# Gated cross-attention block with a quantised FFN: seven instead of six of the eleven products of a pair on Pool

## The reference, cut to what matters

```python
# x: (8, 512, 256); ctx: (8, 512, 256)
x = x + tanh(g_xattn) * attention(layernorm(x), ctx)      # 16 heads of 16, RoPE
xq   = fake_quant(layernorm(x))                           # one scale for the whole tensor
gate = xq @ wq(w_gate).T                                  # (4096, 704)
up   = xq @ wq(w_up).T                                    # (4096, 704)
h    = fake_quant(silu(gate) * up)                        # one scale: max|h| over everything
x    = x + tanh(g_ffn) * (h @ wq(w_down).T)
```

## Time and profile before

| | us |
|---|---|
| median of 3 executions | 604.42 (602.25 to 606.8) |
| the profiled execution, its own time | 602.7 |
| its span, first to last instruction | 600.9 |
| stage 2 of the FFN in it, first silu (514.43) to the last maximum's start (566.93) | 52.5 |
| busy in the span: PE, DVE, ACT, POOL | 565.9, 533.6, 442.1, 253.7 |
| mean granted TensorE clock | 0.995 |

### The profile page before, as it was taken

One profiled execution on the slowest core, in us unless ns is written; L12 is line 12 of the kernel. 1 busy time (PEld: TensorE's weight loads), 2 busy tenths in 40 slices (PEclk: granted clock), 3 DMA queues, 4 the chain that ended last, 5 costly groups with the idle time before them and its releaser, 6 DMA issues. The chain is left out here.

```text
span 600.9 us, 18561 instructions
## 1 busy us (share of the span) xinstructions
PE 565.9 (94%) x6592; PEld 262.3 (44%) x6592; DVE 533.6 (89%) x693; ACT 442.1 (74%) x873; POOL 253.7 (42%) x371
## 2 busy tenths in 40 slices
PE   7999999998899989999999999999999989888985
PEld 3655655233344434444444444444444433333364
DVE  4799989999999979899899899899899775799888
ACT  2667667257777877797797797798798672788694
POOL 8599989701333434214214215215214311665400
PEclk8999999999999999999999999999999999999999
DMA  8759887542332334233333234235222000000035
GB/s 290 242 161 302 244 189 214 139 104 69 73 76 60 73 65 73 53 84 76 53 75 84 53 69 89 53 64 86 62 62 48 3 2 0 2 2 0 0 106 176
DMA packets 61255, 55.21 MB, mean 92 GB/s; under 512 B 11040, under 2 KB 58784, under 8 KB 61216
## 3 DMA queue, kind: packets, MB, share of 16 engines
q1 hardware_dynamic: 61216, 54.70, 36.2%
HBM read 37.62 MB, written 16.78 MB: 91 GB/s over the span
## 5 line engine op out<-in xcount | busy, mean ns | idle before, releaser
L908 ACT ACTIVATE prob<-st_ps 128x512 f32<-128x512 f32 x512 | 280.7, 597 | 71.3 <-PE st_ps L765 64.2
L765 PE MATMUL st_ps<-q,k 98*32 98x512 bf16 x2048 | 178.9, 380 | 6.1 <-ACT prob L908 4.9
L968 DVE TENSOR_REDUCE negm<-xT_ps 128x2 f32<-128x1024 f32 x128 | 154.6, 1207 | 8.4 <-PE xT_ps L338 7.8
L968 DVE TENSOR_REDUCE negm<-v_ps 128x2 f32<-128x1024 f32 x128 | 154.4, 1206 | 6.3 <-PE v_ps L338 6.3
L789 PE MATMUL pv_ps<-prob,v_u 128*32 128x512 f32 x1024 | 132.8, 592 | 0.7 <-ACT prob L908 0.7
L765 PEld LDWEIGHTS st_ps<-q,k 98*32 98x32 bf16 x2048 | 56.9, 95 | 96.3 <-ACT prob L908 41.1
L338 PE MATMUL xT_ps<-k,q 96*32 96x512 bf16 x1024 | 78.4, 379 | 1.4 <-DVE negm L968 1.3
L338 PE MATMUL v_ps<-k,q 96*32 96x512 bf16 x1024 | 78.4, 380 | 1.1 <-DVE negm L968 1.0
L1157 POOL TENSOR_TENSOR msplit<-negm,onesf 128x16 bf16<-128x16 f32 x32 | 7.1, 223 | 129.8 <-DVE negm L968 129.8
L1177 POOL TENSOR_TENSOR normal<-turned,recip 128x256 f32<-128x256 f32 x32 | 19.9, 622 | 78.7 <-DVE recip L982 78.7
L789 PEld LDWEIGHTS pv_ps<-prob,v_u 128*32 128x32 f32 x1024 | 31.8, 110 | 25.8 <-issue 2.0
(11 more groups left out here) (153 smaller groups left out, 807.6 us busy)
## 6 DMA issues: line engine op xcount, KB each, us to landing
qk_parts<-parts SPq DMA_DIRECT2D x96, 128.0 KB, 2.7
k<-qk_parts SPq DMA_DIRECT2D x192, 64.0 KB, 2.7
q<-qk_parts SPq DMA_DIRECT2D x192, 64.0 KB, 3.0
ctx<-in_ctxT SPq DMA_DIRECT2D x8, 512.0 KB, 4.7
X<-in_x SPq DMA_DIRECT2D x8, 512.0 KB, 8.5
out<-X SPq DMA_DIRECT2D x7, 512.0 KB, 2.9
q<-mrow SPq DMA_DIRECT2D x64, 4.0 KB, 2.6
wf<-in_w_down SPq DMA_DIRECT2D x1, 704.0 KB, 5.0
```

What stands on the lines that cost most here:

```text
L765: last = nc.tensor.matmul(score_bank(i)[lo:lo + COLS, :], k6[g][:, h, kt * P + lo:kt * P + lo + COLS], q6[g][:, h, :], start=True, stop=True)
L908: nc.scalar.activation(prob[kt % 2][:, h, :], score_bank(HPU * kt + h)[:], ACT.Exp, scale=SCALE).then_inc(exp_done, 1)
L968: nc.vector.tensor_reduce(negm[g % 2][:, lo:lo + 2], pair[:], op=ALU.max, axis=AX.X, negate=True).then_inc(mx_read, 1)
```

## The change

Slot 4 moves from Pool to DVE, slots 3 and 5 move from DVE to Pool. Pool slots before: 0 2 4 6 8 9; now: 0 2 3 5 6 8 9. DVE slots before: 1 3 5 7 10; now: 1 4 7 10. Over the four pairs that is 24 to 28 copies on ACT, 24 to 28 products on Pool, and 20 to 16 products on DVE.

```diff
         GROUPS = [(s, min(s + 2, SLOTS)) for s in range(0, SLOTS, 2)]
         NG = len(GROUPS)
-        BY_POOL = (0, 2, 4, 6, 8, 9)
+        BY_POOL = (0, 2, 3, 5, 6, 8, 9)
         NPOOL = len(BY_POOL)
         NDVE = SLOTS - NPOOL
```

## The result

Seven Pool slots are slower. The changed kernel takes 607.6 us (median of 17 executions, 605.84 to 609.58), the kernel before 603.06 us in as many beside it: **1.0072 times the time, 95% interval 1.0057 to 1.0088**, or +4.3 us by this ratio. A second set of runs of the same kernel gave 1.0059 (1.0038 to 1.0080). The change is a small loss, within the 1% of the forecast and inside its range; the sum had said +2.2.

The account below looks back on a forecast made before the run. The prediction took a loop through DVE, PE and ACT as the bound, with DVE nearly full but ACT last. Delays of 0.72 + 0.57 + 0.71 + 0.18 = +2.2 us on 604.42 gave 606.6 us, range 601.2 to 609.2.

Parts of the forecast that it names:

- the sum: Added delays at the three joints and the end of pair 3: 0.72 + 0.57 + 0.71 + 0.18 = +2.2 us.
- the loop: Period-setting path: DVE's slot-1 product to `keep_chunk`, PE's slot 5, ACT's silus, PE's next slot 0, ACT's silu of slot 1.
- the first rival: DVE's list sets the pace at the joints; each pair loses 0.67 us, giving 601.7 us; chance 0.15.
- The second, nothing but the copies: Pool's slot 9 ends in time or slot 5's copy finds a gap: 0 to +0.9 us, some 604.9; chance 0.15.
- Slot 3 for slot 4, cost 0: On ACT, slot 3's copy replaces slot 4's; instructions ahead of the silu of slot 5 stay equal in number: 0 us.
- The added copy of slot 5: New on ACT between the silus of slots 5 and 6: +0.33 us in pair 0, +0.18 in each later pair, 0.87 total.
- The wait of the slot-0 copy: At the joints ACT's slot-0 copy waits for Pool's slot 9; silu of slot 1 later by 0.72, 0.57, 0.71 us, shifts included.
- The hand-over: From the end of Pool's slot-9 product to the start of ACT's slot-0 copy: taken as 0.1 us.
- The four instructions a pair that suffer: DVE's scalings and clips, delayed by meeting Pool products, lie in DVE's slack; 0 us added.
- The rule weighed against the trace: DVE 2-port and GpSimd instructions lock each other out for their whole length, so moving work might not help; nothing added.
- The last rival: Shared SBUF access makes DVE the slower bound: 609.3 us if only the scalings wait, 617 if clips do too; chance 0.06.
- the base of 604.42: Median time in us of the three earlier runs of the kernel before, to which the +2.2 was added.

Follow-up runs that it names:

- k1_keep_b: Kernel before (six Pool slots) with `keep_chunk` moved right behind the slot-1 product; stage 49.38 us, ratio 0.9976.
- k2_keep_a: Changed kernel (seven Pool slots) with `keep_chunk` moved right behind the slot-1 product; stage 51.60 us, ratio 1.0012 to the kernel before.
- e1_buf: Changed kernel with four `upb` buffers in place of three; stage 51.53 us, ratio 1.0019 to the kernel before.
- p1_six3: Kernel before with slot 3 on Pool in place of slot 4, still six Pool slots; stage 50.58 us, ratio 0.9992.
- p2_seven4: Kernel before with slot 5 added to Pool's and slot 4 kept there, seven Pool slots; stage 52.47 us, ratio 1.0035.
- e2_clip: Changed kernel with the next chunk's first clip ahead of the maximum after slot 3; stage 52.93 us, ratio 1.0043 to the kernel before.
- e3_both: Changed kernel with four `upb` buffers and the early first clip; stage 51.61 us, ratio 1.0016 to the kernel before.
- k5_six_all: Kernel before (six Pool slots, three buffers) with early `keep_chunk` and early first clip; stage 51.32 us, ratio 1.0016.
- e0_again: Changed kernel run and profiled once more, unedited; stage 53.74 us, ratio 1.0059 to the kernel before.
- k3_all: Changed kernel with four `upb` buffers, early first clip and early `keep_chunk`; stage 51.34 us, ratio 1.0020 to the kernel before.
- k4_keep_buf: Changed kernel with four `upb` buffers and early `keep_chunk`, clip in its old place; stage 49.71 us, ratio 0.9979 to the kernel before.

## Why the prediction was right where it was, and what it missed

The direction, the range and the loop held; what failed is that blocked scalings and clips were put at nothing, which was 0.82 us.

- **The loop.** Right, and shown by k1_keep_b and k2_keep_a: DVE was nearly full and not last. The gain of 2.7 us that DVE's busy share promises did not come; the first rival is out. The second, nothing but the copies, is what e1_buf leaves, +0.91; the changed kernel is 2.22 above that.
- **Slot 3 for slot 4, cost 0.** Right with six Pool slots (p1_six3) and wrong with seven, where the same exchange costs 1.28 us (changed kernel against p2_seven4). The step counted only the ACT instructions ahead of the silu of slot 5. It left out what slots 2 and 3 back to back on Pool can do to DVE: the scaling takes 1.82 us in the changed kernel and 0.74 in p2_seven4. Of the 1.28 the blocked clip, treated further down, is 0.82.
- **The added copy of slot 5, 0.87 us.** Right: 0.91 in e1_buf, pair by pair as worked out.
- **The wait of the slot-0 copy, 2.18 - 0.87 = 1.31 us.** Right: 1.32 between e2_clip and e3_both. The hand-over was 0.07 us a joint shorter than taken; small shifts of about 0.2 us in all, which were not traced, make up for that. That no ACT instruction in the trace is released by Pool holds for this stage only: ahead of it ACT's L306 alone waited seven times for Pool's L287.
- **"The four instructions a pair that suffer lie in DVE's slack ... I add nothing."** This step failed. It counted what a blocked scaling or clip does to DVE's own list, and there it was right in the main: DVE still waited for ACT at every joint, though 0.67 to 0.80 us and not over 1. It left out who waits for the clip. PE's transposes after slot 7 do, ACT's copy behind them does, and ACT is the engine that was last. Measured: 0.82 us. The scaling ahead of the clip had a part in it: at 1.82 us it set the clip later, into Pool's next products, and in e1_buf, at 0.93, the clip got through. The row with the 0.96 us clip was in the earlier trace rows; the question that was not asked of it was which semaphore it raises. The timeline of PE in the kernel before had the answer, in the transposes behind that clip:

```profile
521.23 0.62 PE L1382 MATMUL banks<-identb,wf 128*128 128x128 bf16 x8 [0.18 <-DVE wf L1509]
```

- **The rule weighed against the trace** was the right warning with too small a price. The Trainium skill (SBUF — State Buffer, "SBUF: two separate sides") has the loser fully blocked for the other's whole instruction. The clip of 1.50 us in pair 2 agrees. The scaling of 1.82 us is more than that: it began during Pool's first product and ended after the second, so it was passed over once. The last rival, DVE as the bound by this lock, did not come in the changed kernel, where the lock acted through PE and ACT; it came in k5_six_all.
- **The size.** +2.2 forecast, +3.13 in the stage, +4.3 by the first ratio and +3.6 by the second. The 0.95 between the first two is the blocked clip, 0.82, and 0.1 in small parts. What lies between 3.13 and the ratios is not found; the second interval includes it as nothing, the first leaves 0.3 us. That the time itself, 607.6 us, came within 1.0 of the 606.6 is in part luck: the base of 604.42 was the median of three runs and lay 1.4 above the 603.06 of seventeen, which made up for part of what the sum lacked. And a change below 1%, which the prediction took for too small to be told from none, was told: the interval is some 0.0015 wide to either side.

## What to carry to other kernels

Before work is moved to an engine because the other one is full, follow one period around its loop: what matters is whether a moved instruction lies on it, not the busy share. For each instruction that the move can delay on the way, ask also who waits for its result; slack on its own engine says nothing of that. And where a ring of buffers restarts per turn, count the users modulo its size: seven users on three buffers put the last and the next first on the same one, and a fourth buffer took back 1.3 us and, in this schedule, the collision behind it. A move that is free by itself can cost beside another one, so it is tested in both surroundings.

## What the runs showed of the hardware

- A clip of DVE and a product of Pool that start 0.04 us apart came out in the same order in both profiles of the same program, and the whole stage repeated to 0.01 us. Such a cost is not noise; but a small edit elsewhere turns it (e1_buf), so the sign of an edit of that size can't be carried from one schedule to another: the early clip gave 0.82 us in one kernel and cost 0.08, 1.63 and 1.94 in three others.
- DVE's scaling after slot 2 meets two Pool products back to back in pairs 1 and 2 of nine profiles. In four of them (the changed kernel, e0_again, e2_clip, k2_keep_a) it starts 1.21 or 1.22 us after the start of the first product, waits for both and takes 1.82 or 1.83 us. In five (p1_six3, e1_buf, e3_both, k3_all, k4_keep_buf) it starts 0.83 to 0.88 us after that start, gets in between the two and takes 0.92 to 1.00. No profile has a start between, and what decides it was not isolated.
- ACT started 0.03 or 0.04 us after the end of the Pool product that it had waited for, at all three joints of both profiles of the changed kernel.
